# A decoder of four layers on one Trainium2 core: narrow cross-attentions with norm, query projection and tiles in one block, batch by batch

## What is computed

```
def _L3_xattn_ref(query, key_value, Wq, bq, Wk, bk, Wv, bv, Wo, bo):
    q = (query @ Wq + bq).reshape(B, Nq, H, D).transpose(0, 2, 1, 3)
    k = (key_value @ Wk + bk)...; v = (key_value @ Wv + bv)...
    attn = jnp.einsum('bhqd,bhkd->bhqk', q, k) * scale
    attn = jnp.clip(attn, -CLAMP, CLAMP)
    attn = jax.nn.softmax(attn, axis=-1)
    attn = jnp.where(jnp.any(jnp.isnan(attn)), jnp.asarray(1.0 / Nkv, attn.dtype), attn)
    x = jnp.einsum('bhqk,bhkd->bqhd', attn, v).reshape(B, Nq, Cq)
    return x @ Wo + bo
...
x = x + _L3_xattn_ref(_layernorm(x, axis=-1), ctx_768, ...)
```

## Time and profile before

| | |
|---|---|
| median of 3 runs | 2615.55 us (2613.35 to 2616.92) |
| the profiled execution | 2614.69 us |
| its span, first to last instruction | 2613.0 us |
| PE busy | 2086.1 us (80%) |
| VectorE busy | 1706.7 us (65%) |
| ScalarE busy | 1189.9 us (46%) |
| POOL busy | 588.5 us (23%) |
| mean granted TensorE clock | 0.901 |

### The profile page before, as it was taken

How to read it: one execution, slowest core, us unless ns; L and a number is a source line. 1 busy time by engine, 2 the same in 40 slices (tenths; PEclk the granted TensorE clock), 3 DMA queues, 4 the chain that set the end, 5 groups by cost and what they waited for, 6 DMA issues and landing times. The chain is left out here.

```text
span 2613.0 us, 28449 instructions
## 1 busy us (share of the span) xinstructions
PE 2086.1 (80%) x10279; PEld 1314.2 (50%) x10309; DVE 1706.7 (65%) x2551; ACT 1189.9 (46%) x1889; POOL 588.5 (23%) x346
## 2 busy tenths in 40 slices
PE   5789889695689997969875788888788989283895
PEld 3456557584323324857732444444475654161574
DVE  5555455423677755732177999999965766858675
ACT  2334422110266673511046899999943236412340
POOL 3331122120242212012100675565301210000100
PEclk8889999698799998969988899999989989696896
DMA  6554220343655500034310000000031000000001
GB/s 127 87 87 46 71 97 1 107 155 117 107 73 73 65 1 22 1 110 147 119 59 38 0 1 1 1 1 1 33 102 37 1 0 1 0 8 22 1 1 39
DMA packets 108550, 127.88 MB, mean 49 GB/s; under 512 B 15591, under 2 KB 99444, under 8 KB 107381
## 3 DMA queue, kind: packets, MB, share of 16 engines
q1 hardware_dynamic: 100118, 113.45, 18.8%
q0 software_dynamic: 2880, 7.48, 0.8%
q10 hardware_dynamic: 5408, 5.07, 0.6%
HBM read 92.29 MB, written 33.29 MB: 48 GB/s over the span
## 5 line engine op out<-in xcount | busy, mean ns | idle before, releaser
L3360 DVE TENSOR_TENSOR_SCAN l2s_h<-l2w_aw 128x2048 f32<-128x2048 f32 x64 | 290.1, 4533 | 5.0 <-ACT l2s_rs L3483 5.0
L3288 PE MATMUL l2s_big<-g_xn,g_ident 128*128 128x512 f32 x512 | 258.5, 607 | 11.4 <-ACT g_xn L3476 6.3
L3447 POOL TENSOR_SCALAR l2w_aw<-l2w_aw 128x2048 f32<-128x2048 f32 x64 | 212.2, 3316 | 141.5 <-DVE l2w_aw L3352 136.3
L591 DVE TENSOR_REDUCE l1at_nm<-l1at_s 128x1 f32<-128x512 f32 x256 | 161.9, 683 | 67.6 <-PE l1at_s L441 66.6
L3280 PE MATMUL l2s_c_ps<-g_ident,l2s_h 128*128 128x128 f32 x1024 | 148.9, 279 | 55.8 <-ACT g_xn L3476 36.8
L3280 PEld LDWEIGHTS l2s_c_ps<-g_ident,l2s_h 128*128 128x128 f32 x1024 | 117.2, 142 | 146.5 <-issue 86.9
L691 ACT ACTIVATE g_xn<-l1at_s 128x512 f32<-128x512 f32 x256 | 143.6, 598 | 84.5 <-PE l1at_s L465 83.9
L3476 ACT ACTIVATE g_xn<-l2s_c_ps,l2s_ct 128x512 f32<-128x512 f32 x256 | 162.5, 686 | 16.0 <-PE l2s_c_ps L3280 15.6
L591 DVE TENSOR_REDUCE l0at_nm<-l0at_s 128x2 f32<-128x384 f32 x128 | 69.7, 556 | 90.0 <-PE l0at_s L441 88.9
L3469 ACT ACTIVATE l2w_aw<-l2s_dt,l2w_A 128x2048 f32<-128x2048 f32 x64 | 128.2, 2004 | 0.0
L3288 PEld LDWEIGHTS l2s_big<-g_xn,g_ident 128*128 128x128 f32 x512 | 82.0, 190 | 81.7 <-ACT g_xn L3476 59.1
(11 more groups left out here) (873 smaller groups left out, 4811.9 us busy)
## 6 DMA issues: line engine op xcount, KB each, us to landing
l1f_w<-in_L_ffn_w_dram SPq DMA_DIRECT2D x16, 1024.0 KB, 6.5
l0f_w<-L_ffn_experts_inter_dram SPq DMA_DIRECT2D x7, 1024.0 KB, 5.3
l0f_w<-n_L_ffn_experts_out_dram SPq DMA_DIRECT2D x7, 1024.0 KB, 9.7
l0at_qs<-l0at_parts SPq DMA_DIRECT2D x18, 256.0 KB, 9.1
l0at_ks<-l0at_parts SPq DMA_DIRECT2D x18, 256.0 KB, 17.9
l1at_qs<-l1at_parts SPq DMA_DIRECT2D x18, 256.0 KB, 9.1
l1at_ks<-l1at_parts SPq DMA_DIRECT2D x18, 256.0 KB, 20.8
expert_rows<-g_zeros SPq DMA_DIRECT2D x1, 4096.0 KB, 12.8
```

The lines of the kernel that those rows point to most:

```text
L591: V.tensor_reduce(nm[:, s % 2, qts[0]:qts[-1] + 1, r], s1[:, u % 3, 0:len(qts) * KEYS].rearrange("p (q k) -> p q k", k=KEYS), AX, ALU.max, ...
L3288: nc.tensor.matmul(acc[:, tb, :], ident[:], hCT[:, tb, :], start=n == 0, stop=n == NST - 1).then_inc(acc_done, 1)
L3360: V.tensor_tensor_scan(out=h_all[:, i % 2].rearrange("p c t -> p (c t)"), data0=dA[:, i % 2].rearrange("p c t -> p (c t)"), data1=wd[:, i ...
L3447: nc.gpsimd.tensor_scalar(wd[:, i % 3], wd[:, i % 3], 10.0, -10.0, ALU.min, ALU.max).then_inc(clipped, 1)
```

## The change

In `narrow_cross_attention` the preparation, the block of projections and the loop become one block, which no longer goes through `normalise`. In it

- VectorE normalises the tiles of one batch (`normalised(b)`): batch 0 ahead of all, batch b + 1 at the head of the loop's turn t = 4b, ahead of the shift of t + 2;
- PE transposes them (`turn_xn(b)`, 8 transposes into `t_ps`): batch b + 1 at the end of the turn t = 4b; ScalarE copies them (`copy_xn`), at the end of its own turn; PE projects the queries (`queries(b + 1)`) at the head of the turn t = 4b + 1, and ScalarE keeps them (`keep_queries`);
- the queries of a batch take a place in the alternating use of the score buffer (`slots`), between the scores of tiles t + 1 and t + 2, so that scores wait for the use two places before theirs;
- the values are made behind the queries of batch 0, with one semaphore for all, and VectorE adds their bias ahead of the first shift;
- the keys are spread by 8 scaled copies of ScalarE instead of VectorE's 8 products; POOL clears `vd`;
- POOL adds `bob` batch by batch, each when that batch is normalised. In l3x the sum goes to a buffer of its own (`base`), and x stays as it was until the tile's addition. `scan.make_rows` follows behind in l1x;
- in l3x the loop has no branch. The test for not-a-numbers comes behind the last addition; the replacing block then works from `base`. The loop records the statistics of 14 tiles of x as l1x's does.

The diff, cut (`-` parts are the blocks described above):

```
-            with nc.allow_non_contiguous_dma(reason="bias vectors by feature"):
-                prepare(nc, name + "t", c, loads, jobs)
...
+            slots = [("q", 0)]
+            for t in range(NT):
+                if t % QT == QT - 1 and t + 1 < NT:
+                    slots.append(("q", t // QT + 1))
+                slots.append(("s", t))
+            slot_of = {use: n for n, use in enumerate(slots)}
...
+                @block.gpsimd
+                    clear = Chain(pool, vd_cleared)
+                    clear.step(G.memset(vd[:], 0.0))
...
+                    for b in range(BATCH):
+                        pool.wait_ge(xn_made, (b + 1) * QT)
+                        tiles = slice(b * QT, (b + 1) * QT)
+                        G.tensor_tensor(base[:, tiles, :], x[:, tiles, :], bob[:, None, :].to_broadcast([P, QT, DM]), ALU.add).then_inc(bo_added, 1)
+                    if scan is not None:
+                        scan.make_rows(pool)
...
+                    def take_slot(*use):
+                        n = slot_of[use]
+                        if n < 2:
+                            pe.wait_ge(wt_copied, len(groups))
+                        else:
+                            kind, j = slots[n - 2]
+                            pe.wait_ge(q_kept if kind == "q" else shifted_ready, j + 1)
+                        return s_ps[:, n % 2]
+
+                    def turn_xn(b):
+                        pe.wait_ge(xn_made, (b + 1) * QT)
+                        if b:
+                            pe.wait_ge(pT_copied, (b - 1) * QT + 2)
+                        for kc in range(KC):
+                            for q in range(QT):
+                                ins = nc.tensor.transpose(t_ps[:, (kc * QT + q) * P:(kc * QT + q + 1) * P], xn[:, b * QT + q, kc * P:(kc + 1) * P], ident[:])
+                        ins.then_inc(xn_turned, 1)
...
+                    def queries(b):
+                        slot = take_slot("q", b)
+                        pe.wait_ge(xn_copied, b + 1)
                         for o in range(KC):
                             for k in range(KC):
+                                ins = nc.tensor.matmul(slot[:, o * BANK:(o + 1) * BANK], wq[:, k, o * P:(o + 1) * P], xnT[:, k, b * SEQ:(b + 1) * SEQ],
                                                        start=k == 0, stop=k == KC - 1)
+                        ins.then_inc(q_ready, 1)
...
+                    turn_blocks(nc, pe, groups, weight_banks, ident, loads, loaded, wt_ready, [wt_copied])
+                    turn_xn(0)
+                    keys()
+                    queries(0)
+                    values()
                     scores(0)
                     scores(1)
                     turn(0)
                     for t in range(NT):
+                        b = t // QT
+                        if t % QT == 1 and b + 1 < BATCH:
+                            queries(b + 1)
                         if t + 2 < NT:
                             scores(t + 2)
...
                         weigh(t)
                         if t:
                             outputs(t - 1)
+                        if t % QT == 0 and b + 1 < BATCH:
+                            turn_xn(b + 1)
                     turn_out(NT - 1)
                     outputs(NT - 1)
-                run(pe, program)
+                    if guarded:
+                        pe.wait_ge(nan_found, 1)
+                        pe.wait_ge(y_added, NT)
+                        nc.tensor.matmul(m_ps[:, 0:1], ones[:], anynan[:, 0:1], start=True, stop=True).then_inc(nan_ready, 1)
...
+                @block.vector
+                    normalised(0)
+                    dve.wait_ge(wt_copied, len(groups))
...
+                    for r in range(2):
+                        at = slice(r * CTX, (r + 1) * CTX)
+                        for b in range(BATCH):
+                            V.tensor_tensor(vd[at, b, r::2, 0:D], t_ps[at, b * DM:(b + 1) * DM].rearrange("p (h w) -> p h w", w=D)[:, r::2, :],
+                                            bv[at, r::2, :], ALU.add).then_inc(v_kept, 1)
                     shift(0)
                     shift(1)
                     for t in range(NT):
+                        b = t // QT
+                        if t % QT == 0 and b + 1 < BATCH:
+                            normalised(b + 1)
                         if t + 2 < NT:
                             shift(t + 2)
                         divide(t)
                         if t:
                             add(t - 1)
-                        if t >= 2 and not guarded:
+                        if t >= 2:
                             dve.wait_ge(y_added, t - 1)
                             tile_stats(nc, c, t - 2, t - 1)
                     add(NT - 1)
...
+                @block.scalar
+                    def copy_xn(b):
+                        act.wait_ge(xn_turned, b + 1)
+                        E.copy(xnT[:, :, b * SEQ:(b + 1) * SEQ], t_ps[:].rearrange("p (k n) -> p k n", k=KC)).then_inc(xn_copied, 1)
...
+                    copy_xn(0)
...
+                    spread_keys()
+                    keep_queries(0)
                     exp(0)
                     exp(1)
                     copy_turned(0)
                     for t in range(NT):
+                        b = t // QT
+                        if t % QT == 1 and b + 1 < BATCH:
+                            keep_queries(b + 1)
                         if t:
                             copy_out(t - 1)
                         if t + 1 < NT:
                             copy_turned(t + 1)
                         if t + 2 < NT:
                             exp(t + 2)
+                        if t % QT == 0 and b + 1 < BATCH:
+                            copy_xn(b + 1)
                     copy_out(NT - 1)
```

More of the change, by code:

```diff
@@ L1315, in _ @@
+            slot_of = {use: n for n, use in enumerate(slots)}
+            with nc.allow_non_contiguous_dma(reason="bias vectors by feature"), R.block() as block:
+                from_act = issue_loads(nc, block, loads, loaded)
                 @block.gpsimd
@@ L1593, in program @@
                             ins.then_inc(out_ready, 1)
-                    run(pe, program, True)
+                    run(pe, program)
                 @block.vector
```

401 lines of the change are left out of this document (203 added, 198 removed).

## The result

The changed kernel took 2623.46 us as median of 14 runs (2616.20 to 2629.65), the kernel before beside it 2614.48 us (14 runs, 2609.69 to 2623.45). The ratio is 1.003, 95% interval 1.0018 to 1.0041: some 7.8 us slower (4.7 to 10.7). The forecast was no change, 2614.7 us; the range of 2606 to 2627 holds the median, but the direction was given to a rival with a chance of 0.18.

A forecast was written before the change was run, and what follows sets the result against it. PE bounds the tile loops, while the preparations hold PE idle time and half clock. Terms l1x +1.35, l3x +2.4 and statistics -4.65 sum to -0.9 us, giving a median of 2614.7 us, with a range of 2606 to 2627.

The forecast's parts named there:

- Preparation of l1x, -19.0 and +1.75 for half clock: Before l1x's loop: first scores 19.0 us earlier by the new PE order; half clock, bounds 0 and 3.5, costs 1.75.
- Start of the l1x loop, +1.5: First turns of l1x's loop: value-bias additions on VectorE cost +1.0, transposes and scores at half clock +0.5.
- A batch in l1x, 5.7: l1x loop, three times: transposes 0.9, wait for ScalarE's copy 1.3, queries 3.5, together 5.7 us, in all 17.1.
- l1x, +1.35 in all: Whole l1x stage: -19.0 + 1.75 + 1.0 + 0.5 + 17.1 = +1.35 us.
- Preparation of l3x, -22.4 and "half clock as in l1x, 0 to 3.5: +1.75": Before l3x's loop: first scores 22.4 us earlier; half clock, bounds 0 and 3.5, costs 1.75.
- The rival "no relief at all", 0.10: Both preparations keep all of their half clock, +3.5 us: 2618.2 us; chance 0.10.
- A batch in l3x, 6.3, 7.45, 7.45: l3x loop: 6.5 us per batch plus 0.95 for a clamp held by POOL; 6.3 at batch 1; sum 21.2.
- The open hold of 2.4 us in the range: l3x loop: POOL's addition holding VectorE's small clamps, counted as 2.4 us that might not occur.
- The rival for the falling clock, 0.18: New loop gaps let the clock fall, queries at half rate, 3.5 us per batch: 2625.2 or 2635.7 us; chance 0.18.
- the sign by which I would be wrong: Both loops: among the listed signs of error, the granted clock drops inside the loops; no size given.
- The test behind, +1.75: Behind l3x's last addition: the not-a-number test, reduction to end of flag, adds 1.75 us, all exposed.
- Statistics, -4.65: Stage after l3x: 2 rather than 16 statistics left to make, saving 4.65 us; the other 14 fit VectorE's slack.

The follow-up runs named there:

- only_l1: Changed form in l1x alone, l3x keeping the form of before: +2.6 us against the kernel before (-0.5 to +6.0).
- filled: Changed kernel plus needless matmuls in PE's idle stretches (l3x preparation, both loop starts, ahead of batch 1's queries): about 0 against before (-3.7 to +2.9 us).
- start_only: Changed kernel plus 4 needless matmuls between first scores and first transposes of both loops: +6.5 us against before (+3.1 to +9.9).
- prep_only: Changed kernel plus 4 needless matmuls of 512 columns at the start of l3x: +1.0 us against before (-1.3 to +3.4).
- combined_prep: combined plus 4 needless matmuls of 512 columns at the start of l3x: -13.1 us against before (-16.5 to -9.4).
- base_by_tile: Changed kernel with POOL adding the output bias in l3x one tile at a time, behind each shift: +1.3 us against before (-1.6 to +3.9).
- after_again: The changed kernel unaltered, profiled once more: one execution, l1x 139.8 us, l3x 148.5, last stage 57.2.
- no_stats: Changed kernel without the 14 statistics in l3x's loop; the last stage makes all 16: +11.2 us against before (+7.6 to +15.2).
- only_l3: Changed form in l3x alone, l1x keeping the form of before: +5.8 us against the kernel before (+2.4 to +8.9).
- before_prep: Kernel before plus 4 needless matmuls of 512 columns at the start of l3x: 10.5 us slower than before (+5.5 to +15.7).
- queries_later: Changed kernel with a batch's queries moved behind the next scores and the transposes of the result: 8 us faster than before (-10.7 to -5.2).
- three_moves: Changed kernel with queries behind the next scores, l3x bias added tile by tile, not-a-number test in the loop: -11.5 us against before (-15.2 to -7.8).
- combined: three_moves plus VectorE's first shift ahead of the additions to the values: -2.6 us against before (-5.0 to 0).

## Why the prediction was wrong, point by point

- *Preparation of l1x, -19.0 and +1.75 for half clock.* Measured -19.6 (first scores 25.4 us behind the first load, 45.0 before). The sum was right; the open term was nothing: in after the granted clock is full from the keys on. Whether that is for the barrier or for the 24 transposes that left, no run tells.
- *Start of the l1x loop, +1.5.* From the first scores to the first weighing, before needs 9.1 us (1035.75 to 1044.83), only_l1 11.8 (1012.47 to 1024.26): +2.7. The eight additions lengthen the idle by 1.0 as worked out, but behind it all of the transposes and scores run at half clock, not a part. At full clock the start takes 10.5 (filled, start_only), so the clock is 1.3 to 1.4 of it, where I had 0.5.
- *A batch in l1x, 5.7.* Right where the clock holds, 5.7 to 5.8; 1.5 more for batch 1 in two profiles.
- *l1x, +1.35 in all.* Not refuted: two lengths 4 us apart occur in both forms, and the time of only_l1 is +2.6 (-0.5 to +6.0).
- *Preparation of l3x, -22.4 and "half clock as in l1x, 0 to 3.5: +1.75".* This is the step that failed first, by the size of its clock term. Measured -18.1, not -20.65: first scores 27.3 us behind the first load in after, 24.7 by the sum. I had taken the bound of 3.5 from the mean clock of another stage. In before, the clock rose 11.1 us behind the first load, so that a part of the 32 transposes of `xn` and the first keys ran at full clock; after makes 8 transposes there, the clock rises only at 21.3 us, and transposes, keys, bias and queries all run at half. That the shorter run of transposes is the reason is a guess, and the idle ahead of them (0.52 and 0.55 us in the two profiles with 24.1 and 24.2, 0.80 to 1.06 in the ten with 27.3) is a rival to it that no run tests. Filling shows the whole price: 21.5 us in filled, prep_only and combined_prep, 5.7 to 5.8 less, beyond my bound. The -22.4 fell short besides: for full clock the sum gives 23.0 where 21.5 was measured, in part since its 0.206 us per transpose was read from a stretch at half clock (8 take 1.09, not 1.65).
- *The rival "no relief at all", 0.10.* It came true in l3x, where the half clock stayed and cost 5.7 us instead of its 3.5, and not in l1x.
- *A batch in l3x, 6.3, 7.45, 7.45.* Batches 2 and 3 are 7.5 each, the hold is real and base_by_tile takes it away. Batch 1 is 8.25, 1.7 of it since its queries run at half clock in every profile that leaves this form as it is. (The open hold of 2.4 us in the range was more than the 2 x 0.95 of the text.)
- *The rival for the falling clock, 0.18.* It names the term that the forecast put at nothing, and the sign by which I would be wrong, a clock that drops inside the loops, came. Its mechanism is half right: queries behind a new idle did run at half clock, at 1.5 to 1.7 us per batch, not 3.5, as only a part of the eight matmuls is at half clock, and in one batch of three. What was wrong is the rule that I drew from two rows, that an idle's length decides between 2.81 and 3.12 us. In these runs idles of 1.19 were followed by both levels, of 2.1 by half in l3x and by full in l1x, of 2.94 to 2.99 by full in after and of 2.96 by half in filled. The Trainium skill ("TensorE: Matmul & The Clock Gate", section "HAM oscillation — how this bites in real kernels") describes a kernel in which every burst behind a wait for a transfer, some 3 to 5 us there, starts slow. Of the six batches behind the idles of 1.19 to 2.99 us in after, the trace agrees for batch 1 of either stage, and in after_again for batch 1 of l3x alone.
- *The test behind, +1.75.* 1.83 us from the end of the last addition to the end of the flag, and 0.3 more than before from there to the next statistics: +0.4.
- *Statistics, -4.65.* Right, no_stats.
- *The last stage* had no clock term in the sum. It is 60.2, 57.2 and 60.6 us in the profiles of after, after_again and only_l3, and 57.6, 57.3 and 57.6 in before, only_l1 and before_prep: +2 on average, where it is longer by half clock (12 transposes in 2.79 instead of 1.50).

Together l3x is 3.2 instead of -2.25: 2.5 from the preparation's clock, 1.7 from the clock of batch 1 and 0.3 from its idle, 0.3 at the start, 0.1 in batches 2 and 3, 0.5 behind the loop. With 2 us in the last stage and 0 to 4 in l1x (5.2 to 9.2 in all) that takes in the measured 7.8. That the waits ahead of the queries decide whether the change pays is shown by queries_later, which moves them and keeps everything else, and is 8 us faster than before; three_moves, with two more moves, is 11.5 faster. They don't show that these waits alone make the clock fall: in combined and filled the queries of batch 1 in l3x ran partly at half clock (4.40 and 4.67 us) with no idle ahead of them.

What stays open is where the clock falls in a given execution. It hangs on more than the idle ahead, and it moved between executions of the same code (l1x of after, after_again and only_l1).

## What to carry to other kernels

When work goes from a preparation into a loop bound by TensorE, price the idles it makes there, and put the consumer of a copied tile one independent piece of work behind the transposes: moving it behind 1.6 us of other work was worth some 16 us here, of which the profiles place 6.3 in l3x and 4.6 in l1x against its short form; the rest isn't settled. The granted clock isn't a property of one gap: a term for it needs both ends from the stage itself, and its scatter (4 us for l1x, 3 for the last stage) belongs in the range of every forecast. A long operation of POOL beside clamps on VectorE should be cut into pieces that run behind them.

## What was not expected of the hardware

- The half clock can last 27 us in a loop in which TensorE is busy for 19.66 of 20 us, and four matmuls that ended over 40 us ahead of it are the only difference from a kernel in which this loop runs at full clock from 10 us behind its start on (before_prep, one profile; its time is +5.5 to +15.7).
- Needless matmuls made the changed kernel 8 us faster (filled), and the kernel before 10.5 us slower.
- At the start of l3x's loop half clock cost nothing: 12.4 us from the first scores to the first weighing at either level (after, start_only), as PE waits for ScalarE there.
- The same instructions with the same idle of 1.19 us ahead took 3.67 us in one execution and 5.19 in another.
- A clamp of 128x16 elements took 1.31 instead of 0.17 us beside a POOL addition of 128x1024, and ended with it.
